# Mask sums 128 columns wide instead of 64 in the threshold search of a Mamba / mixture-of-experts / attention block

## The reference

```
x = x + mamba(layernorm(x))
x = x + ffn(layernorm(x))
x = x + attention(layernorm(x))
x = x + ffn(layernorm(x))
```

```
scores = (x_flat @ Wg.T).T                          # 8 experts x 8192 tokens
top_vals, token_idx = jax.lax.top_k(scores, 1024)
token_w = jax.nn.softmax(top_vals, axis=-1)
xg = x_flat[token_idx]
h = silu(xg @ W1.T) * (xg @ W3.T)
y = (h @ W2.T) * token_w
out = zeros.at[token_idx].add(y)
```

## Time and profile before

| what | value |
|---|---|
| median of the three runs | 3172.79 us (3171.89 to 3175.49) |
| the profiled execution | 3173.42 us, of which the span from the first to the last instruction is 3171.6 us |
| PE busy | 2742.0 us, 86% of the span |
| DVE busy | 2231.3 us, 70% |
| POOL busy | 2088.8 us, 66% |
| ACT busy | 1801.6 us, 57% |
| mean granted clock of TensorE | 0.925 of full speed |
| search of stage f: first reduction (L1734) to last | 1764.7 to 1802.1 us |
| search of stage g: first reduction to last | 2736.2 to 2774.1 us |

### The profile page before, as it was taken

How to read it: one execution, slowest core, us unless ns; L and a number is a source line. 1 busy time by engine, 2 the same in 40 slices (tenths; PEclk the granted TensorE clock), 3 DMA queues, 4 the chain that set the end, 5 groups by cost and what they waited for, 6 DMA issues and landing times.

```text
span 3171.6 us, 47750 instructions
## 1 busy us (share of the span) xinstructions
PE 2742.0 (86%) x17112; PEld 1461.6 (46%) x17112; DVE 2231.3 (70%) x2384; ACT 1801.6 (57%) x3171; POOL 2088.8 (66%) x1301
## 2 busy tenths in 40 slices
PE   7788788877887888778866799998999999789999
PEld 3233233333332333233323456655677777455665
DVE  3999999999999999999999632221566666642211
ACT  4777877787877787777775022222555555122222
POOL 3899999999998999999997044444343433134553
PEclk9889898989998899888977899999999999899999
DMA  5556655665566556655562133333111111213442
GB/s 140 130 124 138 146 134 135 141 145 137 129 144 148 135 125 144 150 134 123 137 160 63 58 75 88 67 81 62 42 49 56 49 55 42 78 43 80 93 93 28
DMA packets 225385, 325.19 MB, mean 103 GB/s; under 512 B 40625, under 2 KB 116913, under 8 KB 225026
## 3 DMA queue, kind: packets, MB, share of 16 engines
q1 hardware_dynamic: 200514, 288.04, 36.6%
q0 software_dynamic: 24576, 34.10, 6.3%
q10 hardware_dynamic: 64, 0.02, 0.0%
HBM read 236.08 MB, written 85.95 MB: 102 GB/s over the span
## 4 chain that ended last, share of the span: by engine, by line
PE 53%; DVE 20%; issue 9%; POOL 7%; ACT 6%; DMA 5%; SPq 1%; DVEq 0%; ACTq 0%; POOLq 0%
PE t_wb L2383 9%; PE m_wk L921 9%; PE f_h L1586 7%; PE g_h L1586 7%; DVE m_pair L798 6%; DVE m_hc L798 4%; DMA m_bc<-bcd 4%; PE m_y L1018 4%; DVE m_hc L807 4%; PE g_yp L1600 3%; PE f_yp L1600 3%; POOL m_side L707 3%; POOL m_hc L716 2%; PE t_a_ps L2383 2%; PE t_num L2383 2%
## 5 line engine op out<-in xcount | busy, mean ns | idle before, releaser
L707 POOL TENSOR_TENSOR m_side<-m_du_r,m_bc 128x1024 f32<-128x1024 f32 x384 | 901.2, 2364 | 9.4 <-DMA m_du_r<-ddd 9.4
L716 POOL TENSOR_TENSOR m_hc<-m_hc,m_bc 128x1024 f32<-128x1024 f32 x224 | 527.6, 2358 | 115.3 <-DVE m_hc L798 113.6
L440 ACT ACTIVATE m_pair<-m_delta_r,m_a_neg 128x512 f32<-128x512 f32 x768 | 497.9, 680 | 179.7 <-DVE m_hc L807 94.2
L798 DVE TENSOR_TENSOR_SCAN m_pair<-m_pair,m_side 128x1024 f32<-128x1024 f32 x224 | 511.5, 2283 | 19.0 <-ACT m_pair L440 16.0
L1018 PE MATMUL m_y<-m_hc,m_fold 128*32 128x512 f32 x2048 | 326.9, 714 | 203.2 <-DVE m_hc L807 146.1
L798 DVE TENSOR_TENSOR_SCAN m_hc<-m_pair,m_side 128x1024 f32<-128x1024 f32 x160 | 362.8, 2276 | 10.4 <-ACT m_pair L440 5.9
L807 DVE TENSOR_TENSOR m_hc<-m_pair,m_bc 128x1024 f32<-128x1024 f32 x288 | 350.5, 1217 | 5.7
L921 PE MATMUL m_wk<-m_xnT,m_w_in 128*128 128x512 f32 x488 | 292.1, 729 | 23.3 <-DVE m_delta L783 23.3
L921 PE MATMUL m_wk<-m_xs,m_cw_diag 128*128 128x512 f32 x480 | 226.8, 605 | 10.1 <-ACT m_xs L510 10.1
L1851 DVE TENSOR_TENSOR g_hT<-g_sg,g_h 128x512 f32<-128x512 f32 x64 | 44.0, 687 | 256.7 <-ACT g_sg L1495 256.7
L1851 DVE TENSOR_TENSOR f_hT<-f_sg,f_h 128x512 f32<-128x512 f32 x64 | 44.0, 687 | 254.9 <-ACT f_sg L1495 254.9
(11 more groups left out here) (342 smaller groups left out, 5036.8 us busy)
## 6 DMA issues: line engine op xcount, KB each, us to landing
m_delta_r<-ddd SPq DMA_DIRECT2D x252, 256.0 KB, 6.6
m_du_r<-ddd SPq DMA_DIRECT2D x252, 256.0 KB, 7.5
m_bc<-bcd SPq DMA_DIRECT2D x192, 128.0 KB, 3.0
ddd<-m_delta SPq DMA_DIRECT2D x31, 512.0 KB, 3.0
ddd<-m_du SPq DMA_DIRECT2D x31, 512.0 KB, 3.8
f_w<-in_w SPq DMA_DIRECT2D x24, 512.0 KB, 6.1
g_w<-in_w SPq DMA_DIRECT2D x24, 512.0 KB, 6.0
m_xt<-in_x SPq DMA_DIRECT2D x16, 512.0 KB, 10.0
```

The costliest lines, as they stand in the source:

```text
L440: last = nc.scalar.activation(to, delta_r[:, c % 2, q, :], ACT.Exp, scale=a_neg[:, c * NQ + q, st:st + 1])
L707: nc.gpsimd.tensor_tensor(side[:, un % RING, :, :], du_r[:, c % 2, 2 * h:2 * h + 2, :], bc[:, 0, st:st + 1, :].to_broadcast([P, 2, T]), AL ...
L716: nc.gpsimd.tensor_tensor(hc[:, un % RING, :, :], hc[:, un % RING, :, :], bc[:, 1, st:st + 1, :].to_broadcast([P, 2, T]), ALU.mult).then_i ...
L798: nc.vector.tensor_tensor_scan(to, decay, added, 0.0, ALU.mult, ALU.add).then_inc(S["scan"], 1)
```

## The change

`PART`, the width of a slice, goes from 64 to 128 columns. It is used in `totals_of` and in `holding` only. With 128, a mask takes 4 matmuls of 128 columns instead of 8 of 64, so a round has 12 instead of 24 (each with its own load of the weights `blk_b`), and `tot` holds 3 x 128 = 384 partial sums, which still lie within one row of 512 columns of the PSUM tile `yp`. The reduction L1734 reads 384 columns instead of 192 and still writes three counts. The counts are the same numbers.

```diff
@@ moe
     PAIR = 3
     ROUNDS = 15
-    PART = 64
+    PART = 128
     BIAS = float(1 << 23)
```

## The result

The changed kernel takes 3183.91 us, the median of 8 runs (3181.02 to 3184.77), against 3173.81 us for the kernel before, the median of 8 runs (3171.89 to 3175.49): a ratio of 1.0031, with a 95% interval of 1.0021 to 1.0042. That is 10.1 us slower; forecast were 5.6 us, and 3178.4 us with a range up to 3181.6. The profiled execution took 3183.78 us with a span of 3182.0.

What follows compares the result with a forecast made beforehand. The prediction took each search round to be a loop of dependent steps, 2.63 us long. Reductions at +6.00 us and matmuls at -0.36 us made +5.64 us, so 3178.4 us, 0.18% slower, range 3175.8 to 3181.6.

Steps and rivals of the forecast that it cites:

- What bounds the kernel: In the search, each fine round is one loop of dependent steps, 2.63 us long; the change touches two of them.
- The reduction: In each round's loop, reading 384 columns instead of 192 costs 200 ns more, 557 ns in all.
- The matmuls: After a round's last mask, four matmuls end at 0.397 us where eight ended at 0.410: 13 ns saved per round.
- Which rounds pay in full: In each search, round 0's longer reduction is hidden; from round 1's reduction on, 15 of 16 pay.
- The sum: Over both searches, +6.00 us for the reductions and -0.36 us for the matmuls: together +5.64 us.
- the rival on the weight load: In the rounds, weight loads no longer hide behind the matmul stream: +9.5 us with the reductions, 3182.3 us; chance 0.05.
- What lies behind the search: Work after each search starts 2.8 us later; half-clock stretches may shift either way, about 1.5 us of uncertainty, no direction.
- The prediction's own sign of being wrong: Wrong if a fine round is below 2.75 or above 2.9 us, or the end isn't 5 to 7 us later.
- the clock gives it back: Behind the searches, the shift moves half-clock stretches off TensorE's work: 4.6 us given back, 3173.8 us; chance 0.05.
- the clock did not fall in the fine rounds: Denies a rival: longer PE idle time brings half clock in the fine rounds, 3183.1 us with half of them; chance 0.05.
- the reduction was not cheaper: Denies a rival: the rounds' reduction costs less per column, at the masks' rates, +2.6 to +4.1 us; chance 0.05.

Runs made afterwards that it cites:

- warm_128: The changed kernel with more unread matmuls where TensorE waits behind the search; 3179.47 us, ratio 1.0017 to the kernel before.
- warm_64: The kernel before (64 columns) with more unread matmuls where TensorE waits behind the search; 3174.26 us, ratio 1.0001.
- only_g: The kernel before with 128 columns in the second expert stage (g) only; 3179.45 us, ratio 1.0017.
- split_64: The kernel before (64 columns) with the third mask's sums in another PSUM tile and the first two masks added up early; 3170.41 us, ratio 0.9989.
- wide_again: The changed kernel once more, no further edit, beside the kernel before on another chip; 3196.63 us, ratio 1.0020.
- reduce_twice: The kernel before (64-column matmuls) with the reduction reading the 192 sums twice and the comparison with 2048; 3197.05 us, ratio 1.0018.
- only_f: The kernel before with 128 columns in the first expert stage (f) only; 3192.55 us, ratio 1.0009.
- later_64: The kernel before (64 columns) with six idle mask instructions on VectorE behind round 15 of each search; 3200.10 us, ratio 1.0029.

## Why the prediction was wrong

*What bounds the kernel* held: the round is a loop of dependent steps, and its two changed steps were the right ones. PE's wait grew from 0.35 to 0.55 us a round as said, and the clock in the rounds from 2 on stayed at 1.00, but for the first 0.2 us of round 2.

*The reduction*: +200 ns forecast, 358 to 558 ns measured. (Of the 32 cases before, the shortest took 356 ns, not 357.) The slope of 1.04 ns per column holds from 64 to 384 columns: 225, 290 (128 columns), 358, 558.

*The matmuls*: 13 ns saved per round forecast. From the end of the third mask to the end of the last matmul it was 0.465 us in coarse rounds and 0.468 in fine ones, and is 0.455 and 0.463: 10 and 5 ns saved. The four end 0.403 us after the first starts, not 0.397; their spacing is 58 ns in fine rounds and not 55.6. That makes the sum 0.2 us larger. The figure of 81 ns that the Trainium skill gives for such pairs ("TensorE: Matmul & The Clock Gate", section "Back-to-back issue gap") is not what the trace shows here; its matmul-alone figure of 55.8 is near. By the steps of the rival on the weight load, the figure of 81 ns gives an estimated +9.2 us, not the +9.4 of the prediction.

*Which rounds pay in full*: round 0's reduction is hidden, as said: in g, round 0 to round 1 takes 3.41 us before and after, with a longer reduction in it. In f the half clock in round 1 varies too much from trace to trace to read it.

*The sum*: +5.64 us forecast, 5.8 in the traces, and 5.2 between warm_128 and warm_64, where the clock from the search to the tokens is the same.

*What lies behind the search*: here the prediction failed. It put this term at nothing: a shift of 2.8 us can move work into or out of the stretches at half clock "to either side", "an uncertainty of about 1.5 us on the forecast, not a direction". In f that is so. In g it is a direction: the rise of the clock comes at nearly the same distance behind the start of the search, so the search's length decides, and with 128 columns it ends so that, behind VectorE's scans, during which PE is busy 1.53 of 3.20 us, a stretch at half clock lies right on the path: +1.64 us from last comparison to tokens in each of the four traces with 128 columns in g and no other edit. Before, that place was at full clock in all three traces with 64 columns. The prediction's own sign of being wrong said where to look: the rounds as forecast and the end not 5 to 7 us later. The earlier trace rows held the stretch at that place in f, 1807.9 to 1811.3, and no line for the same place in g. Laid side by side they would have shown that f paid 1.6 us there already and g did not, so that g had it to lose. The rival "the clock gives it back" had the mechanism with the wrong sign.

*The size that remains.* 5.8 and 1.6 are 7.4 us. The three comparisons gave +10.1, +6.2 and +8.2, their mean is 8.2, and each interval is some 3 us wide to either side, so 7.4, a ratio of 1.0023, lies in all three. The forecast of 5.6 is outside the first (from 1.0021, 6.7 us) and inside the other two; it is the traces more than the times that show the missing part. Followed beyond the tokens, g loses more: from last comparison to first SiLU the three traces with 64 columns take 31.53, 30.17 and 30.74 us, the four with 128 take 32.96, 33.80, 32.95 and 33.06, on the mean 2.4 us more. On that way there is a second half-clock stretch, 6.8 us long in all four, and in the three 6.8, 3.4 and 3.4. 5.8 and 2.4 are 8.2 us; but the three traces differ by 1.4 us among themselves, so the second part of it is an estimate. What the 10.1 us of the first comparison hold beyond this stays open, and f's part as well, which meets half clock at that place in some traces of either width. The 5.6 us of only_g are above its 2.9 and 1.6, with 4.5 inside its interval.

*The other rivals*: the clock did not fall in the fine rounds, the weight loads did stay hidden (they are 12 instead of 24 and DVE's wait is the same 0.43), and the reduction was not cheaper.

## What to carry to other kernels

In a loop of two engines, halving the number of matmuls at the same number of columns saves a few ns (5 to 10 a round here), while the reduction behind pays for every further column (200 ns a round here). If the sums come in parts, add up the early ones while the last is still being made, in another PSUM tile as split_64 does (the same tile was not tried). Read the granted clock at each place where PE's work ends the wait, not only in the loop that you change: a loop that ends 3 us later can put a half-clock stretch on the path without itself losing anything. And where two stages run the same code, compare them with each other before the change; a difference at one place is a price that the edit can switch on.

## What the hardware showed that was not expected

TensorE's clock was at 0.50 behind a stretch in which PE was busy for 1.53 of 3.20 us, not idle throughout, and lengthening the work ahead by 0.9 us made the kernel's path behind it 1.65 us shorter. On the chip of wide_again, reduce_twice, only_f and later_64 the kernel before took 3190 us instead of 3173: all four traces from there have 57.4 to 59.1 us from the first SiLU to the ninth in both stages against 52.5 to 53.9 in the others. In wide_again's trace, and for 8.2 to 8.3 us in the other three, ScalarE waits there before L1473 for something that the profile doesn't name:

```profile
1864.89 8.24 another core or an unknown queue
1873.13 0.02 issue
1873.15 0.22 ACT f_sums L1473
```

What it is was not tried.
